# A transformer kernel on one core: the order of work in its segment attention, with the inputs turned one subblock ahead

## The chip, the core and the metric

The kernel runs on one core of a Trainium2 chip. TensorE (PE) does matrix products and transposes, VectorE (DVE), ScalarE (ACT) and GpSimd (POOL) do the work on elements, and SyncE (SP) issues the transfers. Each engine works through its own queue in order and waits on semaphores for the others. The metric is the time of one execution on the device in microseconds, median of three runs.

## The reference

Two sandwiched layers, each an attention and a mixture of experts, on `x` of 2 x 2048 x 128 in float32, every sublayer as `x = x + layernorm(f(layernorm(x)))`. The change touches the first sublayer only, attention in segments of 64 tokens, 16 heads of 64, with 16 persistent keys and values for each head. Shortened:

```python
xn = rmsnorm(x, norm_w)                       # x is layernorm of the input
q, k, v = split(xn @ w_qkv)                   # 16 heads of 64
q, k = rope(q), rope(k)
q_s, k_s, v_s = segments of 64 tokens
k_s = concat(pm_k, k_s); v_s = concat(pm_v, v_s)      # 80 keys
scores = einsum('bhid,bhjd->bhij', q_s, k_s) * 64 ** -0.5, masked causally
attn = softmax(scores)
out = einsum('bhij,bhjd->bhid', attn, v_s) @ w_out + b_out
x = x + layernorm(out)
```

## The kernel before

`local_attention` works through the 4096 tokens in 16 subblocks of 256 tokens (`NSUB`), each two query tiles of 128 tokens, tile 0 and tile 1 (`s` in the code). For a subblock it

- normalises the two tiles of inputs on DVE (`norm`, L336), turns them on PE into PSUM (`turn`, L544), and splits the result into a high part on ACT (`high`, L482) and a low part on DVE (`low`, L341), the buffers `xth` and `xtl`;
- makes four value products of 512 columns (`values_of`, L64 to L66), which ACT copies out of the bank (`values`, L504);
- makes eight projections, q and k of two head pairs at a time (`project`, L64 to L66). DVE multiplies each by cosine and sine (`rope`, L351), SP swaps odd and even rows by a transfer (L325), and POOL adds the two (`add`, L439 for q, L441 for k). A buffer ring of three ties rope `G` to addition `G-3`;
- makes scores for each tile in two halves of eight heads, called quads 0 and 1 (`scores`, L580 and L587). DVE takes their maxima (`maxes`, L358), ACT the exponentials, eight instructions for a quad (`exps`, L488), DVE the sum and its reciprocal (`softmax_back`, L365, L367). The division is shared: DVE does the upper 64 partitions (L371), POOL the lower 64 and the persistent keys (`normalise`, L448, L451), into `pb` and `ppm`;
- does, for each tile, seven *fills* of a PSUM bank (`fill`): transposes of the probabilities (kind `pt`, L605, L607) and products with the values (kind `ot`, L613), in the order pt0, pt1, ot0, pt2, pt3, ot1, pt4, numbered 0 to 6. ACT evacuates each (`evacuate`, L498). An eighth item is the output product (`out_project`, L624, L627). DVE reads it (`out_read`, L378 to L385), POOL takes the power (`power`, L457) and DVE finishes the layer norm and adds it to `X` (`finish`, L390, L394).

The work is a software pipeline written out by hand. In a step, every engine goes through one list in which three subblocks take part: `b` (live: values, projections, first scores), `a` (old, one behind: second scores, softmax, fills of tile 0) and `z` (older, two behind: fills of tile 1). `nxt` is the subblock after `b`, whose inputs are normalised and turned at the end of the step. The 16 fills and output products of a step and the turn share a ring of two banks (`fbank`). `place` and `place_x` number them in PE's order, 17 for a step, and `bank_released` makes each item wait until the item two places before it has been read. So the order on PE, the numbers and the waits hang together.

PE's list in a full step of the kernel before is: fill(z,1) 0; values 0, 1; fill 1; values 2, 3; projection 0; fills 2, 3; projection 1; fill 4; projection 2; fills 5, 6; projection 3; output product (z,1); scores (a,1,0); projection 4; scores (a,1,1); projection 5; fill(a,0) 0; projection 6; fill 1; projection 7; fills 2, 3, 4; scores (b,0,0); fills 5, 6; output product (a,0); turn of `nxt`; scores (b,0,1).

Of the kernel before, what the change touches and what calls it, by code (L numbers as in the profile page):

```python
# [5 lines left out]
F32 = mybir.dt.float32  # L6
# [7 lines left out]
P = 128  # L14
# [78 lines left out]
def local_attention(nc, dr, X, g):  # L93

    m = Mem(nc, "a_")
    with m:
# [125 lines left out]
                    last.then_inc(pm_mm, 1)  # L222

        xn = m.sb("xn", [P, ST, D])
        xth = m.sb("xth", [P, SUB], F32R)
        xtl = m.sb("xtl", [P, SUB], F32R)
        tr = m.sb("tr", [P, TRS, 2, 2, SUB])
        swp = m.sb("swp", [P, SWAPS, 2, SUB])
        qt = m.sb("qt", [P, 2, PAIRS, SUB])
# [45 lines left out]
        def par(n):  # L275
            return n % 2
# [6 lines left out]

        def place(n, s, i):

            return (n + 2) * ITEMS + i if s == 1 else (n + 1) * ITEMS + FILLS + 1 + i

        def place_x(n):
            return n * ITEMS - 1

        def turned_bank(n):
            return fbank[:, place_x(n) % 2, 0:SUB]
# [4 lines left out]
        def bank_released(eng, at):  # L297

            t, k = (at - 2) // ITEMS, (at - 2) % ITEMS
            if k == ITEMS - 1:  # L300
                if 0 <= t + 1 < NSUB:
                    eng.wait_ge(xtl_ready, t + 2)
                return
            n, s, i = (t - 2, 1, k) if k <= FILLS else (t - 1, 0, k - FILLS - 1)
            if 0 <= n < NSUB:
                if i == FILLS:
                    eng.wait_ge(y_read, n * ST + s + 1)
                else:
                    eng.wait_ge(fill_copied, (n * ST + s) * FILLS + i + 1)
# [6 lines left out]
        with nc.Block() as block:  # L316
# [13 lines left out]
            def _(dve):  # L330
# [7 lines left out]

                def low(b):
                    dve.wait_ge(xth_ready, b + 1)  # L340
                    nc.vector.tensor_tensor(xtl[:, :], turned_bank(b), xth[:, :].bitcast(F32),  # L341
                                            ALU.subtract).then_inc(xtl_ready, 1)

                def rope(b, *gs):
# [49 lines left out]
                    nc.vector.tensor_tensor(xs, xs, y[:, s, :], ALU.add).then_inc(y_fin, 1)  # L394

                norm(0)
                for b, a, z, nxt in steps:
                    live, old, older = b is not None, a is not None, z is not None
                    if live:
                        low(b)  # L400
                    if old:
                        maxes(a, 0, 0)
                        maxes(a, 0, 1)
                    if live:
                        rope(b, 0, 1)
                    if old:
                        softmax_back(a, 0)
                    if live:
                        rope(b, 2, 3)
                    if older:  # L410
                        finish(z, 0)
                        out_read(z, 1)
                    if old:
                        maxes(a, 1, 0)
                    if live:
                        rope(b, 4)
                    if old:
                        maxes(a, 1, 1)
                    if live:
                        rope(b, 5, 6, 7)  # L420
                    if nxt is not None:
                        norm(nxt)
                    if older:
                        finish(z, 1)
                    if old:
                        softmax_back(a, 1)
                        out_read(a, 0)

            @block.gpsimd
            def _(pool):  # L430
                def add(b, *gs):
                    for i in gs:
                        G = b * NG + i
                        kind, c = GROUPS[i]
                        pool.wait_ge(rope_mul, 2 * G + 2)
                        pool.wait_ge(swapped[G % SWAPS], 32 * (G // SWAPS + 1))
                        t0, t1 = tr[:, G % TRS, 0, :, :], swp[:, G % SWAPS, :, :]
                        if kind == "q":
                            nc.gpsimd.tensor_tensor(qt[:, par(b), 2 * c:2 * c + 2, :], t0, t1, ALU.add).then_inc(rope_add, 1)  # L439
                        else:  # L440
                            nc.gpsimd.tensor_tensor(kt[:, par(b), 2 * c:2 * c + 2, :, PM:KEYS0],  # L441
                                                    t0.rearrange("p c (a b) -> p c a b", b=SEG),
                                                    t1.rearrange("p c (a b) -> p c a b", b=SEG),
                                                    ALU.add).then_inc(rope_add, 1)

                def normalise(a, s):
                    pool.wait_ge(rden_done, a * ST + s + 1)
                    nc.gpsimd.tensor_tensor(pb[0:64, s, :, 0:SEG], e[0:64, s, :, PM:KEYS0],  # L448
                                            rden[0:64, s, :, None].to_broadcast([64, H0, SEG]),
                                            ALU.mult).then_inc(p_norm, 1)  # L450
                    nc.gpsimd.tensor_tensor(ppm[:, s, :].rearrange("p (h k) -> p h k", k=PM), e[:, s, :, 0:PM],  # L451
                                            rden[:, s, :, None].to_broadcast([P, H0, PM]),
                                            ALU.mult).then_inc(p_norm, 1)

                def power(a, s):
                    pool.wait_ge(y_chain, (a * ST + s + 1) * 3)
                    nc.gpsimd.tensor_tensor(yr[:, s:s + 1], yve[:, s:s + 1], eps[:, 0:1], ALU.pow).then_inc(y_pow, 1)  # L457

                nc.gpsimd.memset(pb[:, :, :, :], 0.0).then_inc(zeroed, 1)
                pool.wait_ge(zeroed, 1)  # L460
                for b, a, z, nxt in steps:
                    live, old, older = b is not None, a is not None, z is not None
                    if older:
                        power(z, 0)
                    if live:
                        add(b, 0, 1)
                    if old:
                        normalise(a, 0)
                    if live:
                        add(b, 2, 3)  # L470
                    if older:
                        power(z, 1)
                    if live:
                        add(b, 4, 5, 6, 7)
                    if old:
                        normalise(a, 1)

            @block.scalar
            def _(act):
                def high(b):  # L480
                    act.wait_ge(xt_mm, b + 1)
                    nc.scalar.activation(xth[:, :], turned_bank(b), ACT.Copy).then_inc(xth_ready, 1)  # L482

                def exps(a, s, j):
                    act.wait_ge(s_max, (a * ST + s) * QUADS + j + 1)
# [21 lines left out]
                high(0)  # L507
                for b, a, z, nxt in steps:
                    live, old, older = b is not None, a is not None, z is not None
                    if older:  # L510
                        evacuate(z, 1, 0)
                    if live:
                        values(b, 0)
                        values(b, 1)
                    if older:
                        evacuate(z, 1, 1)
                    if live:
                        values(b, 2)
                        values(b, 3)
                    if old:  # L520
                        exps(a, 0, 0)
                    if older:
                        evacuate(z, 1, 2, 3)
                    if old:
                        exps(a, 0, 1)
                    if older:
                        evacuate(z, 1, 4, 5, 6)
                    if old:
                        exps(a, 1, 0)
                        evacuate(a, 0, 0)  # L530
                        exps(a, 1, 1)
                        evacuate(a, 0, 1, 2, 3, 4, 5, 6)
                    if nxt is not None:
                        high(nxt)

            @block.tensor
            def _(pe):
# [9 lines left out]
                def values_of(b, c):  # L547
# [6 lines left out]
                        pe.wait_ge(v_copied, b * 2 * ST + c - 1)  # L554
                    ts = slice((c // 2) * P, (c // 2 + 1) * P)
                    vc = slice(2048 + (c % 2) * 512, 2048 + (c % 2) * 512 + 512)
                    matmul_split(nc, pbank[:, c % 2, :], xth[:, ts], xtl[:, ts], wh[:, vc], wl[:, vc]).then_inc(v_mm, 1)

                def project(b, i):
                    if i >= 2:  # L560
# [4 lines left out]
                    for half in range(2):  # L565
                        w0 = (1024 if kind == "k" else 0) + (2 * c + half) * P
                        last = matmul_split(nc, pbank[:, i % 2, half * SUB:(half + 1) * SUB], wh[:, w0:w0 + P],
                                            wl[:, w0:w0 + P], xth[:, :], xtl[:, :])
                    last.then_inc(proj_mm, 1)

                def scores(b, s, j):
# [58 lines left out]
                turn(0)  # L630
                for b, a, z, nxt in steps:
                    live, old, older = b is not None, a is not None, z is not None
                    if older:
                        fill(z, 1, 0)
                    if live:
                        values_of(b, 0)
                        values_of(b, 1)
                    if older:
                        fill(z, 1, 1)
                    if live:  # L640
                        values_of(b, 2)
                        values_of(b, 3)
                        project(b, 0)
                    if older:
                        fill(z, 1, 2, 3)
# [9 lines left out]
                        project(b, 3)  # L655
                    if older:
                        out_project(z, 1)
                    if old:
                        scores(a, 1, 0)
                    if live:  # L660
# [17 lines left out]
                    if old:  # L678
                        fill(a, 0, 5, 6)
                        out_project(a, 0)  # L680
                    if nxt is not None:
                        turn(nxt)
                    if live:
                        scores(b, 0, 1)

# [2783 lines left out]
```

## Time and profile before

| | us |
|---|---|
| runs | 2165.57, 2171.54, 2171.64 (median 2171.54) |
| span of the profiled execution | 2116.7 |
| its own total time | not printed by the page |
| steps of the segment attention | 13 full ones between 88 and 506 |
| busy over the span | PE 1765.5 (83%), DVE 1492.7 (71%), ACT 974.9 (46%), POOL 923.7 (44%) |

The page names one execution. The times of the runs are larger than its span since they hold what lies around it. PE counts as busy while its pipelined products are in flight, so neighbouring rows overlap by about 0.1 us. In a timeline row the bracket tells how long the engine stood idle before it and what released it.

### The profile page before, as it was taken

How to read it: one execution, taken by the hardware profiler on the slowest of the kernel's cores; microseconds unless marked ns; L12 is line 12 of the kernel's file. 1: busy time of each engine (PE TensorE's matmuls, PEld its weight loads, DVE VectorE, ACT ScalarE, POOL GpSimd, SP SyncE). 2: the span in 40 equal slices, each digit the busy share in tenths (PEclk: the TensorE clock that was granted, in tenths of full speed). 3: DMA queues.
4: the chain of work that ended last, by engine and by line, in shares of the span. 5: the costliest groups of instructions: out<-in, count | busy, mean ns of one | idle time of the engine just before them, and what ended most of it. 6: DMA issues, size and time to landing. Idle time of an engine off the chain costs nothing. (4 is left out here: it accounts for less than half of the span.)

```text
span 2116.7 us, 37485 instructions
## 1 busy us (share of the span) xinstructions
PE 1765.5 (83%) x13932; PEld 1331.8 (63%) x13932; DVE 1492.7 (71%) x3418; ACT 974.9 (46%) x2147; POOL 923.7 (44%) x637
## 2 busy tenths in 40 slices
PE   3788888888769999889999779965899779978993
PEld 2677777777635666446665557644688558767883
DVE  5678777787477887387787478878787776864234
ACT  2455545545415565525556345432333244325664
POOL 3455555565314566514555336654000220165644
PEclk9999999999859999979999889988899889988997
DMA  5112112111010000000000023319600000016763
GB/s 172 66 63 81 51 71 76 56 71 66 16 42 1 2 1 1 1 1 1 1 2 1 1 71 101 95 60 229 149 1 1 0 1 1 8 38 194 213 219 118
DMA packets 78469, 124.11 MB, mean 59 GB/s; under 512 B 11824, under 2 KB 43440, under 8 KB 77776
## 3 DMA queue, kind: packets, MB, share of 16 engines
q1 hardware_dynamic: 73744, 112.31, 17.1%
q0 software_dynamic: 4544, 9.41, 1.3%
q8 instruction: 111, 1.82, 0.4%
q14 instruction: 70, 0.57, 0.1%
HBM read 59.19 MB, written 28.94 MB: 42 GB/s over the span
## 5 line engine op out<-in xcount | busy, mean ns | idle before, releaser
L1089 POOL TENSOR_TENSOR mb_psum<-mb_pt 128x1024 f32<-128x1024 f32 x112 | 267.0, 2387 | 291.4 <-ACT mb_pt L1049 290.5
L1049 ACT ACTIVATE mb_pt<-mb_stb 128x1024 f32<-128x1024 f32 x256 | 249.2, 1021 | 143.2 <-PE mb_stb L1170 142.7
L914 DVE TENSOR_REDUCE mb_mxp<-mb_p1b 128x1 f32<-128x512 f32 x352 | 231.2, 684 | 50.2 <-PE mb_p1b L1154 46.3
L351 DVE TENSOR_TENSOR ma_tr<-ma_pbank,ma_cs 128x512 f32<-128x512 f32 x256 | 161.7, 683 | 91.4 <-PE ma_pbank L66 81.6
L488 ACT ACTIVATE ma_e<-ma_sbank,ma_mx 128x80 f32<-128x80 f32 x512 | 120.3, 385 | 99.0 <-DVE ma_mx L358 99.0
L2466 PE MATMUL mc_pv<-mc_pt,mc_v 128*128 128x256 f32 x544 | 148.2, 398 | 17.3 <-DVE mc_pt L2269 17.3
L1154 PE MATMUL mb_p1b<-mb_ks,mb_qs 96*128 96x512 f32 x352 | 151.3, 473 | 7.0 <-DVE mb_qs L907 3.3
L439 POOL TENSOR_TENSOR ma_qt<-ma_tr,ma_swp 128x512 f32<-128x512 f32 x64 | 82.3, 1289 | 167.8 <-DMA ma_swp<-ma_tr 167.7
L1170 PE MATMUL mb_stb<-mb_qs,mb_ks 98*128 98x512 f32 x512 | 143.8, 402 | 0.8 <-ACT mb_pt L1049 0.8
L2269 DVE COPY mc_pt<-mc_tb 128x512 f32<-128x512 f32 (+1 forms) x144 | 94.0, 658 | 61.5 <-PE mc_tb L2451 61.1
L1181 PE MATMUL mb_pvb<-mb_pt,mb_v 128*32 128x256 f32 x2048 | 137.0, 385 | 0.0
L1593 POOL TENSOR_TENSOR mb_hh<-mb_hh,mb_gb 128x512 f32<-128x512 f32 x64 | 98.7, 1545 | 82.8 <-DVE mb_hh L1610 55.4
L1756 POOL TENSOR_TENSOR mc_frs<-mc_fve,mc_half 128x4 f32<-128x4 f32 x8 | 8.1, 1012 | 275.5 <-DVE mc_fve L1740 275.4
L914 DVE TENSOR_REDUCE mb_mxp<-mb_misc 128x1 f32<-128x512 f32 x160 | 109.2, 682 | 22.0 <-PE mb_misc L1154 22.0
L2466 PEld LDWEIGHTS mc_pv<-mc_pt,mc_v 128*128 128x128 f32 x544 | 96.8, 196 | 35.3 <-DVE mc_pt L2269 25.8
L1170 PEld LDWEIGHTS mb_stb<-mb_qs,mb_ks 98*128 98x128 f32 x512 | 94.2, 189 | 33.2 <-issue 12.3
L498 ACT ACTIVATE ma_pt<-ma_fbank 128x512 f32<-128x512 f32 (+1 forms) x160 | 94.2, 590 | 42.2 <-PE ma_fbank L605 41.8
L64 PE MATMUL ma_pbank<-ma_xth,ma_wh 128*128 128x256 f32 x256 | 85.6, 334 | 30.0 <-DVE ma_tr L351 30.0
L1154 PEld LDWEIGHTS mb_p1b<-mb_ks,mb_qs 96*128 96x128 f32 x352 | 67.4, 199 | 67.8 <-DVE mb_mxp L914 48.2
L448 POOL TENSOR_TENSOR ma_pb<-ma_e,ma_rden 64x1024 f32<-64x1024 f32 x32 | 90.1, 2817 | 31.6 <-DVE ma_rden L367 31.6
L613 PE MATMUL ma_fbank<-ma_pt,ma_v 128*64 128x128 f32 x1024 | 73.6, 287 | 35.3 <-ACT ma_pt L498 35.2
L441 POOL TENSOR_TENSOR ma_kt<-ma_tr,ma_swp 128x512 f32<-128x512 f32 x64 | 83.6, 1316 | 39.0 <-DMA ma_swp<-ma_tr 34.6
(404 smaller groups left out, 4767.2 us busy)
## 6 DMA issues: line engine op xcount, KB each, us to landing
ma_swp<-ma_tr SPq DMA_DIRECT2D x256, 128.0 KB, 2.0
md_wslot<-d_weights SPq DMA_DIRECT2D x39, 516.0 KB
d_xs<-mw_blank SPq DMA_DIRECT2D x1, 16899.0 KB, 72.3
mb_gb<-b_gates SPq DMA_DIRECT2D x64, 256.0 KB, 3.2
md_xs<-d_xs SPq DMA_DIRECT2D x39, 131.0 KB, 3.3
md_work<-d_ret SPq DMA_DIRECT2D x8, 512.0 KB, 5.4
mg_X<-x SPq DMA_DIRECT2D x4, 512.0 KB, 9.8
ma_cs<-cs SPq DMA_DIRECT2D x1, 2048.0 KB, 9.9
```

The source lines that it names most:

```text
L351: nc.vector.tensor_tensor(tr[:, G % TRS, part, :, :], pbank[:, i % 2, :].rearrange("p (c t) -> p c t", c=2), cs[:, b // 2, part, None, :]. ...
L488: nc.scalar.activation(e[:, s, slot, :], sbank[:, 2 * j + k // 4, k % 4 * KEYS0:(k % 4 + 1) * KEYS0], ACT.Exp, bias=mx[:, s, slot:slot + 1 ...
L498: nc.scalar.activation(to[:, 4 * q:4 * q + nh, :], filled_bank(a, s, i)[:, 0:nh * P].rearrange("p (a b) -> p a b", b=P), ACT.Copy).then_in ...
L914: nc.vector.tensor_reduce(mxp[:, r // NCH, r % NCH:r % NCH + 1], pass_bank(r), AXX, ALU.max).then_inc(p1_max, 1)
L1049: nc.scalar.activation(pt[:, T % RING, :, :].rearrange("p (b h) q -> p b (h q)", b=2), stb[:, 2 * (i % 2):2 * (i % 2) + 2, :], ACT.Exp, sc ...
L1089: nc.gpsimd.tensor_tensor(psum[:, n % SUMS, :, :], pt[:, T % RING, :, :], pt[:, (T + 1) % RING, :, :], ALU.add).then_inc(summed, 1)
L1154: nc.tensor.matmul(pass_bank(r), qs[V % 3][0:QROWS, h, t * P:(t + 1) * P], ks[0:QROWS, c * BLK:(c + 1) * BLK], start=True, stop=True).then ...
L1170: last = nc.tensor.matmul(stb[:, 2 * (i % 2) + hp, :], ks[:, i * P:(i + 1) * P], qs[U % 3][:, 2 * hp:2 * hp + 2, :].rearrange("p h q -> p ...
L1181: last = nc.tensor.matmul(pvb[h * DK:(h + 1) * DK, 0:UQ], v1[:, i, :], pt[:, T % RING, h, :], start=(i == 0), stop=(i == KT - 1), skip_gro ...
L1593: nc.gpsimd.tensor_tensor(hh[:, t % HR, :], hh[:, t % HR, :], gb[:, q % GBR, :], ALU.mult).then_inc(gated, 1)
L2269: nc.vector.tensor_copy(pt[:, K % 2, 0:wd], tb[:, K % 2, 0:wd]).then_inc(pt_copied, 1)
L2466: last = nc.tensor.matmul(pv[:, 0:HC * P], v[:, t, :], pt[:, K % 2, a * HC * P:(a + 1) * HC * P], start=(t == 0), stop=(t == r))
```

## The change

The buffers `xth` and `xtl` are doubled, and the parity of the subblock chooses the half. The turn of the next subblock goes from the end of the step to the place behind the output product of tile 1, and its number in the ring with it. The order on each engine changes:

- PE: fill(z,1) 0 stands behind values 0 and 1, and fill 1 behind values 2 and 3; the turn behind the output product (z,1). The rest stays.
- ACT: evacuations 0 and 1 of (z,1) behind the copies of values 1 and 3; evacuation 4 ahead of the exponentials (a,0,1); the high part ahead of the exponentials (a,1,0).
- DVE: the norm of `nxt` and the finish of (z,0) behind the first maxima; rope 2 ahead of the softmax part of (a,0); the low part behind the read of (z,1).
- POOL: addition 2 ahead of normalising (a,0).

```diff
-        xth = m.sb("xth", [P, SUB], F32R)
-        xtl = m.sb("xtl", [P, SUB], F32R)
+        xth = m.sb("xth", [P, 2, SUB], F32R)
+        xtl = m.sb("xtl", [P, 2, SUB], F32R)
...
-            return (n + 2) * ITEMS + i if s == 1 else (n + 1) * ITEMS + FILLS + 1 + i
+            return (n + 2) * ITEMS + i if s == 1 else (n + 1) * ITEMS + FILLS + 2 + i
 
         def place_x(n):
-            return n * ITEMS - 1
+            return (n - 1) * ITEMS + FILLS + 1
...
             t, k = (at - 2) // ITEMS, (at - 2) % ITEMS
-            if k == ITEMS - 1:
+            if k == FILLS + 1:
                 if 0 <= t + 1 < NSUB:
                     eng.wait_ge(xtl_ready, t + 2)
                 return
-            n, s, i = (t - 2, 1, k) if k <= FILLS else (t - 1, 0, k - FILLS - 1)
+            n, s, i = (t - 2, 1, k) if k <= FILLS else (t - 1, 0, k - FILLS - 2)
... (DVE)
                 norm(0)
+                low(0)
                 for b, a, z, nxt in steps:
-                    if live:
-                        low(b)
                     if old:
                         maxes(a, 0, 0)
                         maxes(a, 0, 1)
+                    if nxt is not None:
+                        norm(nxt)
+                    if older:
+                        finish(z, 0)
                     if live:
-                        rope(b, 0, 1)
+                        rope(b, 0, 1, 2)
                     if old:
                         softmax_back(a, 0)
                     if live:
-                        rope(b, 2, 3)
+                        rope(b, 3)
                     if older:
-                        finish(z, 0)
                         out_read(z, 1)
+                    if nxt is not None:
+                        low(nxt)
                     if old:
                         maxes(a, 1, 0)
...
                         rope(b, 5, 6, 7)
-                    if nxt is not None:
-                        norm(nxt)
                     if older:
                         finish(z, 1)
... (POOL)
-                        add(b, 0, 1)
+                        add(b, 0, 1, 2)
                     if old:
                         normalise(a, 0)
                     if live:
-                        add(b, 2, 3)
+                        add(b, 3)
... (ACT)
-                    if older:
-                        evacuate(z, 1, 0)
                     if live:
                         values(b, 0)
                         values(b, 1)
                     if older:
-                        evacuate(z, 1, 1)
+                        evacuate(z, 1, 0)
                     if live:
                         values(b, 2)
                         values(b, 3)
+                    if older:
+                        evacuate(z, 1, 1)
                     if old:
                         exps(a, 0, 0)
                     if older:
-                        evacuate(z, 1, 2, 3)
+                        evacuate(z, 1, 2, 3, 4)
                     if old:
                         exps(a, 0, 1)
                     if older:
-                        evacuate(z, 1, 4, 5, 6)
+                        evacuate(z, 1, 5, 6)
+                    if nxt is not None:
+                        high(nxt)
                     if old:
                         exps(a, 1, 0)
                         evacuate(a, 0, 0)
                         exps(a, 1, 1)
                         evacuate(a, 0, 1, 2, 3, 4, 5, 6)
-                    if nxt is not None:
-                        high(nxt)
... (PE)
-                    if older:
-                        fill(z, 1, 0)
                     if live:
                         values_of(b, 0)
                         values_of(b, 1)
                     if older:
-                        fill(z, 1, 1)
+                        fill(z, 1, 0)
                     if live:
                         values_of(b, 2)
                         values_of(b, 3)
+                    if older:
+                        fill(z, 1, 1)
+                    if live:
                         project(b, 0)
...
                         out_project(z, 1)
+                    if nxt is not None:
+                        turn(nxt)
...
                         out_project(a, 0)
-                    if nxt is not None:
-                        turn(nxt)
```

## Rows read from the trace of the kernel before

**Rows 1.** Windows between input copies: bounds, length, busy PE, PEld, DVE, ACT, POOL, clock, DMA

```profile
88.00:120.00 32.00, 28.62 (x358) 24.32 (x354) 24.43 (x42) 16.95 (x52) 17.54 (x14) 0.95 0.18 68
...
376.70:409.30 32.60, 27.00 (x350) 22.98 (x350) 25.75 (x41) 16.86 (x51) 18.10 (x15) 1.00 0.18 66
...
474.50:506.10 31.60, 27.08 (x350) 23.07 (x350) 25.54 (x42) 16.92 (x52) 17.19 (x15) 1.00 0.18 68
```

**Rows 2.** Waits from 88 to 506 us: total, times, longest

```profile
PE ma_fbank L613 <- ACT ma_pt L498: 23.4, 25, 1.3
...
PE ma_fbank L605 <- POOL ma_ppm L451: 14.2, 11, 1.6
```

**Rows 3.** Timeline of PE, one step: start, busy, what, idle before and its releaser

```profile
376.25 0.38 PE L544 MATMUL ma_fbank<-mg_ident,ma_xn 128*128 128x128 f32 x2
...
379.05 0.66 PE L605 MATMUL ma_fbank<-mg_ident,ma_pb 128*128 128x128 f32 x4 [1.61 <-POOL ma_ppm L451]
379.46 0.48 PE L64 MATMUL ma_pbank<-ma_wh,ma_xth 128*128 128x512 f32 x1
...
380.94 0.60 PE L605 MATMUL ma_fbank<-mg_ident,ma_pb 128*128 128x128 f32 x4
...
382.92 0.39 PE L64 MATMUL ma_pbank<-ma_xth,ma_wh 128*128 128x256 f32 x1
...
388.65 1.09 PE L613 MATMUL ma_fbank<-ma_pt,ma_v 128*64 128x128 f32 x16 [1.30 <-ACT ma_pt L498]
...
390.67 1.95 PE L624 MATMUL ma_fbank<-ma_wout,ma_ot 128*128 128x128 f32 x16
...
393.00 0.33 PE L580 MATMUL ma_sbank<-ma_mask,mg_identb 64*64 64x320 bf16 x4
```

**Rows 4.** Timeline of DVE, the same step

```profile
377.64 0.42 DVE L341 TENSOR_TENSOR ma_xtl<-ma_fbank,ma_xth 128x256 fp32r<-128x256 f32 x1
...
383.93 1.29 DVE L351 TENSOR_TENSOR ma_tr<-ma_pbank,ma_cs 128x512 f32<-128x512 f32 x2 [4.42 <-PE ma_pbank L66]
...
388.05 1.49 DVE L365 TENSOR_REDUCE ma_den<-ma_e 128x16 f32<-128x1280 f32 x1 [0.51 <-ACT ma_e L488]
...
389.86 2.17 DVE L371 TENSOR_TENSOR ma_pb<-ma_e,ma_rden 64x1024 f32<-64x1024 f32 x1
...
395.04 0.28 DVE L378 TENSOR_TENSOR ma_y<-ma_fbank,ma_bout 128x128 f32<-128x128 f32 x1
...
395.98 0.82 DVE L358 TENSOR_REDUCE ma_mx<-ma_sbank 128x8 f32<-128x640 f32 x1
...
402.74 1.97 DVE L336 TENSOR_SCALAR ma_xn<-mg_X,ma_mean,ma_xsc 128x128 f32<-128x128 f32 x2
```

**Rows 5.** Timeline of ACT, the same step

```profile
380.44 1.30 ACT L504 ACTIVATE ma_v<-ma_pbank 128x512 f32<-128x512 f32 x2
...
383.46 1.84 ACT L488 ACTIVATE ma_e<-ma_sbank,ma_mx 128x80 f32<-128x80 f32 x8
...
386.09 1.93 ACT L488 ACTIVATE ma_e<-ma_sbank,ma_mx 128x80 f32<-128x80 f32 x8
387.77 0.74 ACT L498 ACTIVATE ma_pt<-ma_fbank 128x512 f32<-128x512 f32 x1
```

**Rows 6.** Timeline of POOL, the same step

```profile
387.40 1.27 POOL L439 TENSOR_TENSOR ma_qt<-ma_tr,ma_swp 128x512 f32<-128x512 f32 x1 [7.90 <-DMA ma_swp<-ma_tr]
389.67 1.27 POOL L439 TENSOR_TENSOR ma_qt<-ma_tr,ma_swp 128x512 f32<-128x512 f32 x1 [1.00 <-DMA ma_swp<-ma_tr]
...
393.76 0.61 POOL L451 TENSOR_TENSOR ma_ppm<-ma_e,ma_rden 128x256 f32<-128x256 f32 x1
```

**Rows 7.** All instructions of L336, of L371 and of L448: duration ns min/median/max

```profile
L336 DVE TENSOR_SCALAR ma_xn<-mg_X,ma_mean,ma_xsc x32: 334/700/3545, 29.8 to 500.0; 128x128 f32<-128x128 f32 x32
...
L371 DVE TENSOR_TENSOR ma_pb<-ma_e,ma_rden x32: 1221/1418/2179, 69.2 to 561.8; 64x1024 f32<-64x1024 f32 x32
...
L448 POOL TENSOR_TENSOR ma_pb<-ma_e,ma_rden x32: 1892/2896/2942, 70.1 to 561.9; 64x1024 f32<-64x1024 f32 x32
```

## The prediction before the run

> **What bounds the kernel now.** I read four views, in this order. First the windows, cut at the ScalarE copies of the turned input, one per step. Between 88.0 and 506.1 us there are 13 full steps, 418.1 us together, 32.16 on average; most take 32.6, the others 31 to 32 [rows 1]. In none is an engine full: in the step from 376.7, PE works 27.0 us of 32.6 and DVE 25.8. A pipeline like that is bound by a loop of waits. PEclk is 1.00 there, so the clock doesn't explain it.
>
> Then the waits [rows 2]. PE waits for POOL's normalised probabilities, 14.2 us in 11 waits, and for ScalarE's copies of transposed probabilities, 23.4 in 25. The timeline places them. I count from A, the start of the turn at 376.25 us, which follows the output product. The next A is 32.6 later.
>
> - Turn and last scores end at 377.44 (A+1.19); then PE idles 1.61 until the first fill of tile 1 at A+2.80. Value products, a fill between them, and projection 0, which starts at A+6.67, follow [rows 3].
> - DVE, idle 4.42 meanwhile, starts rope 0 at A+7.68 [rows 4].
> - ScalarE ends the exponentials of tile 0, quad 1, at 388.02 (A+11.77) [rows 5]. That frees DVE's softmax back part at A+11.80; its multiply into `pb` takes 2.17 because POOL is adding at that moment [rows 4, 6]. Rope 2 and 3, finish and read follow, and the maxima of tile 1, quad 0, start at A+19.73.
> - From there DVE, ScalarE and PE hand over with small gaps to the next A, 408.85-395.98 = 12.87 later.
>
> DVE also works 1.97 on the next inputs' norm at 402.74, before the softmax part whose result the first fill awaits [rows 4].
>
> The 31.6 steps are those in which that first fill comes about 1 us sooner. So in a long step the loop runs: A, first fill, values, projection 0, rope 0, softmax back, maxima (1,0), exponentials, fills of tile 0, output product, A.
>
> **The change, part by part.** Durations and pitches (start to start) are those of the rows; the clock starts at A again. Nothing is added: the buffers double, the instructions are the same.
>
> *Opening of PE.* The turn goes from here (0.38 busy) to behind the output product of tile 1, and the first fill goes behind two value products. Scores run 0 to 0.81, values 0 and 1 to 2.29 (379.46 to 380.94 is 1.48 for two), fill 0 to 2.70, values 2 and 3 to 4.18, fill 1 to 4.59. Projection 0 is ready 1.01 after its start (382.92 to 383.93): A+5.60, against A+7.68. Copies don't hold it up: the first two end 2.28 after the first value product starts (A+3.09), the next two at A+4.98, and each product awaits a copy that ended before.
>
> Does the first fill still wait? Its data are ready at A+2.80 less hand-over today. With the norm (1.97) gone from in front of that softmax part they come near A+0.9; they are wanted at A+2.29. Margin 1.4.
>
> *ScalarE.* After the copies: evacuation 1 to 5.57, eight exponentials to 7.25 (the next starts 1.68 after them, 386.09 to 387.77), evacuations 2 and 3 to 8.2 (0.95 for two today, 383.46 + 1.68 = 385.14 to 386.09). Evacuation 4 now stands before the second eight. PE: fill 2 starts when evacuation 1 ends, 5.65 to 6.68, fill 3 to 7.09, projection 1 ready at 8.10, fill 4 behind it at 8.65. So evacuation 4 runs 8.69 to 9.29, the exponentials 9.15 to 11.05. They end 0.7 sooner than now, not 2.08: that is the price of evacuation 4 in front. From A+1.79 to A+11.05 ScalarE would work 2.4 + 3.0 + 3.6 = 9.0 of 9.26 us, nearly full. In exchange fill 5 no longer waits 1.30 for evacuation 4 behind the exponentials [rows 3, 5]: the output product of tile 1 can start at 11.6 instead of A+14.42.
>
> *DVE.* Rope 0 at 5.63, rope 1 at 8.12, rope 2, now before the softmax part, 9.42 to 10.7. It fits in the wait for the exponentials, so it costs nothing; without that cover, 1.24. Softmax back from 11.08, its multiply at 12.89. POOL adds rope 0 from 9.1 (lag 3.47, 383.93 to 387.40), rope 1 from 11.5, rope 2 from 12.85. The multiply again meets an addition: 2.17, so 15.1; the ends are 1.22 and about 2.5 (1.22 behind a whole addition of 1.27) [rows 6, 7]. I take 2.17, the row with the same collision. Rope 3 to 16.3. Finish, 0.58 until the read, has gone; reading the output product takes 0.94 (395.04 to 395.98), the low part of the turned inputs 0.42. Maxima (1,0) start at A+17.65, 2.1 sooner.
>
> *What was moved to the opening*, norm and finish of tile 0, follows the first maxima, A+2.6 to A+3.9; rope 0 wants DVE at 5.63. Cover 1.7 us. POOL is idle then, so the norms should take 0.33 rather than up to 1.4 each [rows 7]; even two at 1.4 fit, nearly.
>
> *The moved turn.* Output product 11.6 to 13.93 (390.67 to 393.00 is 2.33), turn to 14.3, ScalarE's high part to 14.7. Waiting instructions: the high part, with exponentials (1,0) queued behind it, wanted at 18.5; the low part on DVE, with the maxima (1,0) behind it, reached at 17.2. Margin 2.5. Fill 1 (A+4.2) now waits for DVE's read of the last output product, done near A+0.4: no cost.
>
> *POOL and SP.* POOL normalises tile 0 behind the third addition: 14.1 to 17.6 (2.90 and 0.61). PE asks at 17.7 and would next wait for rope 4 anyway until 19.6: cover 2.0. SP's swaps keep their order and lag; an addition of rope G-3 frees each slot in time, as before.
>
> *Sum.* The stretch from the maxima on keeps its 12.87: the new step is 17.65 + 12.87 = 30.5, for all steps alike, since the late first fill of the 32.6 us steps no longer decides. Per step 32.16 - 30.5 = 1.65; 13 steps 21.4. The step after 506.1, and the one behind it in which evacuation 4 frees the last output product sooner, I count as one gain each (estimate): 3.3. The head, two steps without a full pipeline, 0. Sum 24.7. The profiled span goes from 2116.7 to about 2092. The page prints only the span; the runs lie 48.9 to 54.9 above it, their median 54.8. I subtract from the median: 2171.5 - 24.7 = 2147.
>
> **A rule weighed.** The multiply takes 1.22 to 2.18 and its POOL partner 1.89 or 2.9, so one stands while the other works [rows 6, 7]. The Trainium skill, "SBUF — State Buffer", section "Who interferes with whom", says that a VectorE instruction with two SBUF inputs contends with a GpSimd instruction that reads SBUF, and that whichever starts first holds the shared ports for its whole length. By that rule this change is delicate: if the third addition starts first, the multiply takes up to 2.49, and the sum is 14 x 0.32 = 4.5 us worse, 2151; if the multiply starts first it runs free, which is the first rival below, 2134. The trace agrees with it in both lengths.
>
> **Rivals.**
> 1. *The multiply gets ahead of the third addition.* My sum has them 0.04 us apart (12.89 and 12.85), far below its accuracy. The multiply then takes 1.22, 0.95 less, and POOL's wait is covered. 14 steps: 13 more, 2134. Against: all POOL additions slide with the same ropes, and in 12 of the 13 steps today's multiply of tile 0 takes over 2.1 (one such row stands). Chance 0.13.
> 2. *Only the late first fill goes.* Every step becomes what the short ones are, 31.6, and no more, because exponentials (0,1) or the evacuations bind at the old distance. 0.56 in each of 15 steps: 8.4, so 2163. For: that is a time the trace shows. Against: the turn and fill 0 leave PE's opening as well. Chance 0.15.
> 3. *ScalarE's queue binds, and the kernel is slower.* One place: evacuation 4 in front of exponentials (0,1). It waits for fill 4, which stands on PE behind projection 1 and fill 2, which wait for evacuations 1 and 2 of the same queue. Any lateness goes round this ring and straight into the softmax part. A slip of the exponentials' start from 9.15 by 1.65 takes the whole gain; from there on it is a loss, and at 2.3 it is 15 x 0.65 = 10 us: 2181. For: the queue is 97% full by my sum. Against: its copies take 0.60 in every row and depend on nothing that got later; they would need a third more. Slower 0.08; a slip of 1.2 to 2.1, no measurable change, 0.09.
> 4. *The change doesn't do what it says*, since the turn arrives late and DVE stands at the low part: from an output product at 14.1 on, 1 us for each. It starts at A+14.42 today, so even with evacuation 4 of no use it would cost only 0.3 a step. It is inside my range.
>
> **How the numbers follow.** The forecast has 0.55, with its own range 2138 to 2158 (0.6 to 2.2 us a step). Rival 1 gives 2134, rival 2 2163 to 2166. The range is 2133 to 2166. A difference of 0.3%, 6.5 us, is about what a measurement of this kernel can tell from none: faster means under 2165. Faster: 0.55 + 0.13 + two thirds of 0.15 = 0.78; same: the rest of rival 2 and 0.09 = 0.14; slower 0.08.
>
> **What would show it.** The 13 steps all near 30.5 us, without the 31.6/32.6 mix. PE's wait for POOL's `ppm` before the fills gone. The norms at 0.33, right behind the first maxima. DVE's softmax multiply at 2.17 (1.22 is rival 1). PE's 1.30 wait for evacuation 4 gone, output product of tile 1 near A+11.6. Wrong would be: ScalarE idle before evacuation 4 by over 1 us, DVE's wait before the sum of exponentials over 1 us (rival 3), DVE waiting at the low part (rival 4), or a PEclk under 0.97 in these steps.

## The result, and the profile after

| | before | changed |
|---|---|---|
| runs | 2170.86 us (2165.57 to 2171.64) | 2132.09 us (2124.59 to 2136.96) |
| ratio | | 0.9822, 95% interval 0.9804 to 0.9841 |
| first attention ends, in the trace | 581.7 | 541.9 |
| mean of the 12 steps between rope 0 of subblocks 3 and 15 | 32.31 | 29.47 |

The change is worth 39 us, and the trace has all of it, 39.8 us, in the part that was changed. Forecast were 2147 and a range from 2133: right in sign, too small, and 0.9 us outside the range. The number that came is that of the first rival, 2134.

One warning on the spans: the changed kernel's profiled span is 2135.2 us, longer than the 2116.7 of before. The profiled run took 2136.96, so only 1.8 us lie around a span. The profile of before was of an execution some 50 us quicker than the timed ones. Its last two parts, which the change doesn't touch, have the lengths that the quicker chips show (last section). Within the first attention the two traces compare. So the reason given ahead of the prediction, that the runs are longer than the span by what lies around it, was wrong.

Windows of the changed kernel, cut at the input copies as in [rows 1], with the same columns:

```profile
101.80:131.10 29.30, 27.20 (x348) 23.22 (x346) 24.31 (x41) 16.79 (x51) 18.09 (x15) 1.00 0.20 74
307.70:337.40 29.70, 27.61 (x352) 23.58 (x350) 24.11 (x42) 16.78 (x51) 18.57 (x15) 1.00 0.19 72
425.90:455.30 29.40, 27.33 (x348) 23.29 (x347) 23.81 (x42) 16.79 (x51) 18.26 (x15) 1.00 0.20 74
```

Steps are nearly all alike, 29.4, and PE works as long as before in each, 27.2 to 27.6 us, now 93% of it. DVE needs 23.8 to 24.3 in these three windows, against 25.8 in the one from 376.7 before, for the same instructions: less of its time is spent waiting on POOL inside an instruction. Of the waits of [rows 2] PE's for `ppm` fell from 14.2 to 2.5 us, the one for the copies from 23.4 to 7.5 (here from 102 to 455 us, 12 steps against 13):

```profile
PE ma_fbank L615 <- ACT ma_pt L500: 7.5, 12, 1.0
...
PE ma_fbank L607 <- POOL ma_ppm L453: 2.5, 3, 1.2
```

Now one step in time. The line numbers of ACT, POOL and PE are 2 higher than before. A, where the last scores start on PE, is 323.54 (352.90, the next one, less 29.36). DVE first; its rows answer to [rows 4]:

```profile
326.06 0.59 DVE L336 TENSOR_SCALAR ma_xn<-mg_X,ma_mean,ma_xsc 128x128 f32<-128x128 f32 x2
...
329.05 1.29 DVE L351 TENSOR_TENSOR ma_tr<-ma_pbank,ma_cs 128x512 f32<-128x512 f32 x2 [1.81 <-PE ma_pbank L66]
331.56 2.48 DVE L351 TENSOR_TENSOR ma_tr<-ma_pbank,ma_cs 128x512 f32<-128x512 f32 x4 [1.22 <-PE ma_pbank L66]
334.37 1.49 DVE L365 TENSOR_REDUCE ma_den<-ma_e 128x16 f32<-128x1280 f32 x1 [0.32 <-ACT ma_e L490]
...
336.18 1.22 DVE L371 TENSOR_TENSOR ma_pb<-ma_e,ma_rden 64x1024 f32<-64x1024 f32 x1
...
339.90 0.82 DVE L358 TENSOR_REDUCE ma_mx<-ma_sbank 128x8 f32<-128x640 f32 x1
```

PE, ACT and POOL in the same step, the answers to [rows 3], [rows 5] and [rows 6]:

```profile
332.74 1.09 PE L615 MATMUL ma_fbank<-ma_pt,ma_v 128*64 128x128 f32 x16
...
334.97 2.02 PE L626 MATMUL ma_fbank<-ma_wout,ma_ot 128*128 128x128 f32 x16
...
352.90 0.33 PE L582 MATMUL ma_sbank<-ma_mask,mg_identb 64*64 64x320 bf16 x4
...
355.21 0.60 PE L607 MATMUL ma_fbank<-mg_ident,ma_pb 128*128 128x128 f32 x4
```

```profile
332.00 0.60 ACT L500 ACTIVATE ma_pt<-ma_fbank 128x512 f32<-128x512 f32 x1 [0.30 <-PE ma_fbank L607]
332.49 1.85 ACT L490 ACTIVATE ma_e<-ma_sbank,ma_mx 128x80 f32<-128x80 f32 x8
```

```profile
336.27 2.26 POOL L443 TENSOR_TENSOR ma_kt<-ma_tr,ma_swp 128x512 f32<-128x512 f32 x1
...
353.25 0.61 POOL L453 TENSOR_TENSOR ma_ppm<-ma_e,ma_rden 128x256 f32<-128x256 f32 x1
```

The point to see is the pair 336.18 and 336.27. DVE's multiply starts 0.09 us before POOL's addition 2. It runs free, 1.22 us, and it is the addition that takes 2.26 instead of 1.27. In [rows 4, 6] it was the other way round.

### The profile page after: what moved, and what is told of

Its sections match the earlier page's. It is cut to its first block and busy times, and to the rows that moved or that the text cites. A ratio compares the mean times of both kernels' runs of the same rounds, so it can differ in the third digit from the quotient of the medians.

```text
span 2135.2 us, 37484 instructions
## 1 busy us (share of the span) xinstructions
PE 1782.7 (83%) x13932; PEld 1340.9 (63%) x13932; DVE 1469.6 (69%) x3418; ACT 973.7 (46%) x2147; POOL 920.9 (43%) x637
## 5 line engine op out<-in xcount | busy, mean ns | idle before, releaser
L3326 PE MATMUL md_bk<-md_xT,md_wslot 128*128 128x256 f32 x312 | 99.5, 404 | 13.7 <-issue 10.9
L3112 POOL DMA_INDIRECT d_ret<-md_ys,md_home x78 | 76.8, 985 | 78.4 <-DVE md_ys L3245 65.0
L443 POOL TENSOR_TENSOR ma_kt<-ma_tr,ma_swp 128x512 f32<-128x512 f32 x64 | 96.8, 1516 | 23.6 <-DMA ma_swp<-ma_tr 18.6
L3056 ACT ACTIVATE md_a<-md_bk,md_wslot 128x256 f32<-128x256 f32 x156 | 70.6, 477 | 73.8 <-PE md_bk L3326 26.3
```

The source lines that it names most:

```text
L3326: nc.tensor.matmul(ub[:, c, :], wslot[:, j % WRING, c * P:(c + 1) * P], xT[:, j % 2, :], start=True, stop=True).then_inc(up_mm, 1)
```

## The experiments

The experiments ran on four chips, each beside the kernel before; ratios compare, microseconds across the two kinds of chip (last section) don't. "Step" is the mean of the same 12 steps as above, in one trace; in brackets the commonest single step, or the range of most.

| kernel | step | ratio (interval) |
|---|---|---|
| before | 32.31 (32.6) | 1 |
| changed; again in E12 | 29.47; 29.43 (29.36) | 0.9822; 0.9819 (0.9789 to 0.9849) |
| E1 multiply waits for addition 2 | 33.30 (32.5 to 33.6) | 1.0101 (1.0074 to 1.0128) |
| E9 multiply 0.4 us later | 30.62 (30.6) | 0.9884 (0.9856 to 0.9913) |
| E2 norm back | 29.71 (29.8) | 0.9853 (0.9832 to 0.9873) |
| E3 rope 2 back | 30.67 (30.55) | 0.9914 (0.9894 to 0.9935) |
| E4 evacuation 4 back | 29.52 (29.5) | 0.9830 (0.9810 to 0.9851) |
| E7 turn back | 29.82 (29.8) | 0.9834 (0.9785 to 0.9882) |
| E13 fills back | 29.93 (29.7) | 0.9864 (0.9826 to 0.9902) |
| E6 before, addition 1 held | 33.73 (32.6 to 34.6) | 1.0100 (1.0048 to 1.0152) |
| E10 before, finish ahead | 31.33 (30.9 to 32.0) | 0.9950 (0.9920 to 0.9979) |
| E11 before, both | 30.52 (30.0 to 31.1) | 0.9892 (0.9864 to 0.9920) |
| E8, E14 fill 1 ahead | 28.84; 28.88 (28.75) | 0.9754; 0.9779 |
| E15 and low part behind | 28.86 (28.75) | 0.9784 (0.9739 to 0.9829) |

The intervals of E2, E4, E7 and E13 overlap with that of the changed kernel. What is said of them rests on the steps, which the two traces of the changed kernel repeat to 0.04 us.

**E1.** One wait in front of the multiply of tile 0.

```diff
+                    if s == 0 and a + 1 < NSUB:
+                        dve.wait_ge(rope_add, (a + 1) * NG + 3)
```

> The changed kernel, with one wait more: DVE's multiply of tile 0 into pb waits until POOL has ended addition 2 (rope 2). So the collision that I had forecast is brought back as a full wait. Theory (this multiply stands on the loop that sets the step; it ran free at 1.22 us, and that is the 1 us a step that my sum lacked): the multiply starts near A+14.1 instead of A+12.63, the step goes from 29.4 to 30.8 us, the kernel from 2132 to about 2152. Rival (this place has slack and the gain came from elsewhere): step 29.4, time 2132.

The time was 2188 us, a loss of 56 and not 20. DVE and then POOL:

```profile
373.45 2.84 DVE L373 TENSOR_TENSOR ma_pb<-ma_e,ma_rden 64x1024 f32<-64x1024 f32 x1 [1.50 <-POOL ma_kt L445]
```

```profile
372.08 1.27 POOL L445 TENSOR_TENSOR ma_kt<-ma_tr,ma_swp 128x512 f32<-128x512 f32 x1
373.31 1.90 POOL L452 TENSOR_TENSOR ma_pb<-ma_e,ma_rden 64x1024 f32<-64x1024 f32 x1
```

When the wait lets DVE go, POOL has begun to normalise 0.14 us before, and the multiply stands behind that as well. Counted from rope 0 (364.85), it ends at 11.44; in the changed kernel (329.05) at 8.35. That is 3.09 later, and the step without another collision went from 29.36 to 32.5, by 3.1. So the direction of the theory holds, one for one; its size missed since I had not looked at what POOL does next.

**E5 and E9.** The multiply is delayed by small instructions that read the sums and write a spare tile: one in E5, three in E9.

```diff
+                    if s == 0:
+                        for k in range(3):
+                            nc.vector.reciprocal(rdx[:, k, :], den[:, s, :])
```

> The changed kernel, with one small DVE instruction more (the reciprocal of tile 0's sums once again into a spare tile, 0.29 us with its gap) right in front of the multiply of tile 0. In the changed kernel the multiply starts at A+12.63 and POOL's addition 2 at A+12.73. Theory (who starts first decides, and my forecast had the wrong one first by 0.1 us): the multiply now asks after addition 2 has begun and takes 2.2 to 2.3 us, 1.22 before; the step goes from 29.4 by 0.29 + 1.0 to 30.7, near the 30.5 of my forecast, and the kernel by 14 x 1.3 = 18 us to 2150. Rival (the overlap is not decided so sharply, DVE has precedence): multiply 1.22, step 29.65, +4 us.

E5 didn't bring the collision about: ratio 0.9835 (0.9785 to 0.9886), step 29.51. The extra instruction overlaps the one before and delayed the multiply by 0.1 us, not 0.29. DVE stayed first, by 0.02 us. DVE, then POOL:

```profile
367.57 1.22 DVE L374 TENSOR_TENSOR ma_pb<-ma_e,ma_rden 64x1024 f32<-64x1024 f32 x1
```

```profile
367.59 2.35 POOL L446 TENSOR_TENSOR ma_kt<-ma_tr,ma_swp 128x512 f32<-128x512 f32 x1
```

> The changed kernel, with three small DVE instructions in front of the multiply of tile 0 (the reciprocal of the sums three times into a spare tile). One such instruction delayed the multiply by 0.1 us only, and it was still first, by 0.02 us. Three should delay it by 0.5, behind the start of POOL's addition 2. Theory (who starts first decides): the multiply takes about 2.0 us, ends 1.1 to 1.3 later than in the changed kernel, step 30.6, the kernel +16 us. Rival (DVE has precedence, or the overlap is graded): multiply 1.22, step 29.36 + 0.5 = 29.9, +7 us.

In E9 the multiply starts 0.21 us behind the addition. DVE, then POOL:

```profile
347.42 2.14 DVE L375 TENSOR_TENSOR ma_pb<-ma_e,ma_rden 64x1024 f32<-64x1024 f32 x1
```

```profile
347.21 1.26 POOL L447 TENSOR_TENSOR ma_kt<-ma_tr,ma_swp 128x512 f32<-128x512 f32 x1
```

Step 30.6, as the theory had it; the rival's 29.9 is out. Counted from rope 0, the multiply starts 0.33 us later than in the changed kernel and ends 1.25 later, and the step is 1.25 longer: 0.33 is the delay, 0.92 the collision. In time, on one chip, E9 took 2146.1 us and the changed kernel (E12) 2130.4, where the theory had 16 us. The run holds a control of its own: where two multiplies happened to get through in 1.22 us the step took 29.7 and 30.2, though a step of 31.5 followed the second. This kernel, the changed one with the collision of my forecast and the multiply at about the start that I had given it, has the step of my forecast (30.5).

**E2, E3, E4, E7, E13** undo one part each.

E2 (DVE) and E3 (DVE, and the same on POOL):

```diff
+                norm(1)
...
-                    if nxt is not None:
-                        norm(nxt)
...
                         rope(b, 5, 6, 7)
+                    if b is not None and b + 2 < NSUB:
+                        norm(b + 2)
```

```diff
-                        rope(b, 0, 1, 2)
+                        rope(b, 0, 1)
...
-                        rope(b, 3)
+                        rope(b, 2, 3)
```

> The changed kernel, with DVE's norm of the inputs back behind rope 7, ahead of finish and softmax part of tile 1 (for the subblock after next, so the early turn stays). Theory (the move of the norm freed the first fill): POOL's results for the first fill come near A+2.9 instead of A+0.96, PE wants them at A+2.3: a wait of 0.6 us comes back, step 30.0, kernel +9 us. Rival (the norm's place is covered on both sides, the gain is all of the rope 2 and softmax part): step 29.4, no change.

> The changed kernel, with rope 2 on DVE and addition 2 on POOL back behind the softmax part of tile 0. Theory (rope 2 fills the wait for the exponentials, so its place is worth its whole length): DVE idles about 1.5 us before the sum of exponentials and does rope 2 on the loop, step 29.4 + 1.2 = 30.6, kernel +17 us; the multiply stays near 1.22 to 1.3, since addition 1 ends about when it starts. Rival (only the multiply's luck matters): the multiply free as well, step 29.4. A third reading, that addition 1 now collides with the multiply: multiply about 2.2, step 31.5.

The norm's place is worth 0.25 (mean) to 0.45 us (commonest step), under the 0.6 expected, though more than the rival's nothing. Rope 2's place is worth its length: 1.19 in the commonest step. DVE idles 19.7 us in 13 waits before the sum of exponentials, 1.5 each, where it idled 0.32.

E4 (ACT) and E7 (turn, high and low part, ring numbers as before; the turn stands here for all three):

```diff
-                        evacuate(z, 1, 2, 3, 4)
+                        evacuate(z, 1, 2, 3)
...
-                        evacuate(z, 1, 5, 6)
+                        evacuate(z, 1, 4, 5, 6)
```

```diff
                         out_project(a, 0)
+                    if nxt is not None:
+                        turn(nxt)
```

> The changed kernel, with evacuation 4 of tile 1 back behind the exponentials of tile 0, quad 1. Theory: two ends meet here. Exponentials end 0.6 us sooner, but DVE then starts only 0.3 sooner, behind rope 2; the output product of tile 1 starts at A+12.65 instead of A+11.4 and its result is read by DVE at A+15.1, when DVE comes anyway. Step 29.4 within 0.2, kernel the same. Rival (the early evacuation is what brought the gain): step over 30, kernel +8 us or more. Other rival (it costs, as my working had it, 0.6 us of exponentials): step 29.1 or less, -4 us.

> The changed kernel, with the turn, its high part on ScalarE and low part on DVE back where they stood before, at the end of the step (ring numbers too), the norm and all other orders as changed. Theory: the turn (0.31) stands on PE's opening again and the value products wait for the low part, which DVE has ready near A+1.9 rather than for nothing from A+0.85: projection 0 comes 1.0 to 1.1 us later, step 30.5, kernel +14 us. Rival (the turn early is worth only its own 0.31, since the first fill fills the gap): step 29.7, +4 us.

E4: no change in time, 0.15 in the step, as the theory forecast, but not for its reason. DVE, then POOL:

```profile
337.39 1.59 DVE L371 TENSOR_TENSOR ma_pb<-ma_e,ma_rden 64x1024 f32<-64x1024 f32 x1
```

```profile
336.61 1.29 POOL L441 TENSOR_TENSOR ma_qt<-ma_tr,ma_swp 128x512 f32<-128x512 f32 x1 [0.56 <-DMA ma_swp<-ma_tr]
337.92 2.21 POOL L443 TENSOR_TENSOR ma_kt<-ma_tr,ma_swp 128x512 f32<-128x512 f32 x1
```

The multiply starts 0.42 us sooner after rope 0 than in the changed kernel, 6.71 instead of 7.13. There it meets the last 0.5 us of addition 1, takes 1.59, and ends at 8.30 instead of 8.35. So a collision eats what the later evacuation gives the exponentials, and E4 doesn't say what evacuation 4 in front costs by itself.

E7 lost 0.44, nearer to the rival's answer: rope 0 comes 0.7 us later after the output product, but without the low part the stretch between the multiply and the maxima is 0.3 shorter. I had added up only one side in this expectation.

E13 puts fill(z,1) 0 ahead of the value products and fill 1 between them, with their evacuations:

> The changed kernel with the first two fills of tile 1 (and their evacuations) back where they stood: fill 0 ahead of the value products, fill 1 between them. The early turn and all else stay. Theory (with the norm out of the way POOL's results come 1.4 us before PE wants them, so the spreading only permutes items of equal length): step 29.4 within 0.2, no change. Rival (the spreading brought part of the gain, since evacuation 0 now stands ahead of the value copies and the third value product waits): step 29.8 or more, +5 us.

0.33 us in the commonest step, 0.5 on the mean, and PE's waits for `ppm` are back in some: 7.9 us in 15 waits (2.5 in 3). The theory's "no change" is out. The mean step, 29.93, is the rival's, the commonest, 29.7, just under it: the spreading by itself is worth a little.

**E6, E10, E11** do parts in the kernel before. E6 on POOL, E10 on DVE, E11 both:

```diff
-                        add(b, 0, 1)
+                        add(b, 0)
+                    if old:
+                        pool.wait_ge(p_norm_high, a * ST + 1)
+                    if live:
+                        add(b, 1)
```

```diff
                         maxes(a, 0, 1)
+                    if older:
+                        finish(z, 0)
...
-                        finish(z, 0)
                         out_read(z, 1)
```

> The kernel before, with POOL's addition 1 held until DVE's multiply of tile 0 has ended (a wait on its semaphore; order otherwise the same). Theory (in the kernel before this multiply stood on the loop as well, and its collision cost 0.95 us in nearly every step): multiply 1.22 instead of 2.17, the step 32.28 to 31.3, the kernel -12 to -13 us, about 2156. Rival (before, the loop ran through other places, the collision was covered): step 32.3, no change, or slower because addition 1 comes 1.4 us later.

E6 was slower, 1.0100, against the theory. The rival had allowed for it, by the later addition; the rows show more than that. DVE, then POOL:

```profile
401.30 1.22 DVE L371 TENSOR_TENSOR ma_pb<-ma_e,ma_rden 64x1024 f32<-64x1024 f32 x1
402.55 2.48 DVE L351 TENSOR_TENSOR ma_tr<-ma_pbank,ma_cs 128x512 f32<-128x512 f32 x4
404.95 0.86 DVE L390 TENSOR_SCALAR ma_y<-ma_y,ma_ymv,ma_yr 128x128 f32<-128x128 f32 x1
405.84 3.08 DVE L394 TENSOR_TENSOR mg_X<-mg_X,ma_y 128x128 f32<-128x128 f32 x1
```

```profile
402.60 1.27 POOL L439 TENSOR_TENSOR ma_qt<-ma_tr,ma_swp 128x512 f32<-128x512 f32 x1 [2.54 <-DVE ma_pb L371]
403.83 1.90 POOL L448 TENSOR_TENSOR ma_pb<-ma_e,ma_rden 64x1024 f32<-64x1024 f32 x1
405.69 0.62 POOL L451 TENSOR_TENSOR ma_ppm<-ma_e,ma_rden 128x256 f32<-128x256 f32 x1
406.27 2.50 POOL L441 TENSOR_TENSOR ma_kt<-ma_tr,ma_swp 128x512 f32<-128x512 f32 x2
```

The multiply is free, but POOL's work is now one row without a pause, 402.60 to 408.77, and the finish, 0.6 us alone, sits in it for 3.9 us. That gives a new theory for each of two runs:

> The kernel before with one part of the change: DVE's finish of tile 0 (two instructions, 0.6 us) behind the first maxima instead of between rope 3 and the read of the output product. Theory (the stretch from the multiply to the maxima of tile 1 is on the loop, 1 for 1): step 32.28 to 31.65, the kernel -8 us. Rival (in the kernel before, other waits cover it): no change.

> The kernel before with POOL's addition 1 held until the multiply of tile 0 has ended, and DVE's finish of tile 0 behind the first maxima. Held alone, the addition made the multiply free but the finish met POOL's unbroken row of normalise and additions and took 3.9 us instead of 0.6. Theory (the two collisions are the whole reason): with the finish out of the way the step is 32.28 - 0.95 - 0.6 = 30.7, the kernel about -20 us. Rival (holding the addition costs of itself, by later additions): step over 32.

E11 bears the theory out: 30.52 against 30.7, and 22 us less, while the edits alone gave +25 and -9. With the finish out of POOL's row, the held addition is good for 0.8 us a step (31.33 to 30.52). E10 gained 0.98, more than the finish's 0.6. The traces show where the rest lies: the maxima (1,0) follow rope 0 by 11.45 us instead of 12.03 (medians of 12 steps), and in the opening too POOL's `ppm` is ready 0.6 sooner behind the output product, 2.41 instead of 3.01, and rope 0 with it.

**E12** is the changed kernel once more.

> The changed kernel again, so that it stands beside the others on one chip. Every theory: ratio to the kernel before 0.982 within 0.003, step 29.4 to 29.5.

**E8, E14, E15**, further than the change. E8 and E14 are one kernel; PE, then ACT:

```diff
-                        fill(a, 0, 0)
+                        fill(a, 0, 0, 1)
```

```diff
-                        evacuate(a, 0, 0)
+                        evacuate(a, 0, 0, 1)
                         exps(a, 1, 1)
-                        evacuate(a, 0, 1, 2, 3, 4, 5, 6)
+                        evacuate(a, 0, 2, 3, 4, 5, 6)
```

> A trial to go further: the changed kernel, with fill 1 of tile 0 ahead of projection 6 on PE and its evacuation ahead of the exponentials of tile 1, quad 1, on ScalarE. Theory (the tail of the loop runs exponentials (1,1), evacuation 1, fill 2, ..., output product): fill 2 no longer waits for evacuation 1 behind the exponentials, starts 0.5 us sooner, behind projection 7; step 28.9, kernel -7 us, 2125. Rival (the exponentials, 0.5 later, or projection 7 bind instead): step 29.4, no change.

> The trial with fill 1 of tile 0 and its evacuation ahead once more, to stand on one chip with the others: step 28.7 to 28.9, ratio 0.976 to the kernel before.

E15 moves DVE's `low(nxt)` behind `maxes(a, 1, 0)` on top of it.

> The same with DVE's low part of the turned inputs behind the maxima of tile 1, quad 0, instead of ahead of them. Theory (the stretch from the multiply to these maxima is on the loop 1 for 1): 0.33 us less, step 28.4, the kernel -4 to -5 us against the trial before. Rival (exponentials (1,0), or rope 4 behind the low part, bind at the old time): step 28.75.

Fill 1 ahead takes 0.6 us off the step on two chips. The ratios 0.9754 and 0.9779 lie below the changed kernel's 0.9822 and 0.9819, which ran on other chips, but their intervals overlap or nearly touch; the step is the sharper sign. With E15, which equals it, it is the fastest version here. E15 gave nothing: with fill 2 no longer behind the exponentials, PE waits 0.95 us for rope 5 ahead of projection 7, and rope 5 comes at the same time wherever the low part stands before it. In the changed kernel the stretch to the maxima counted one for one when it grew (E1, E3, E9) and when it shrank (the 0.3 us of E7); in E8's kernel shrinking it no longer helps.

## Why the prediction was wrong

The loop was the right one, and its steps can be set against the trace (A = 323.54):

| | forecast | trace |
|---|---|---|
| rope 0 | A+5.63 | A+5.51 |
| evacuation 4, exponentials (0,1) | 8.69, 9.15 | 8.46, 8.95 |
| output product, tile 1 | 11.6 | 11.43 |
| `ppm` of tile 1 ready, fill 0 wants it | 0.9, 2.29 | 0.96, 2.31 |
| multiply starts; addition 2 starts | 12.89; 12.85 | 12.64; 12.73 |
| multiply takes | 2.17 | 1.22 |
| maxima (1,0) | 17.65 | 16.36 |
| step | 30.5 | 29.36 |

**The step that failed** is "The multiply again meets an addition: 2.17, so 15.1". The mechanism was named, and rival 1 gave its price and the time that was measured. What was wrong is the choice between two starts that my own sum had 0.04 us apart. It came out 0.09 the other way, E5 left DVE first by 0.02 with no loss, and in E9, with DVE 0.21 behind, the step was 30.6. That shows both that the order of the starts decides and that this one length is the shortfall: 0.95 of the 1.2 us a step. The other 0.25 is the multiply's earlier start, from exponentials that began 0.2 sooner than in my sum. (The maxima came 1.29 sooner than forecast in all, and the stretch behind them took 13.00 instead of 12.87.) The 12.85 was itself loosely worked: with my lag of 3.47 behind rope 2 at 9.42, addition 2 starts at 12.89, exactly with the multiply. My argument against rival 1, that today's multiply collides in 12 of 13 steps, carried nothing: then it met addition 1, now addition 2, with another lag. It deserved near one half, and the range a lower end.

**Right**, by its own step: the first fill's wait went, its margin is 1.35 us (forecast 1.4), and E2 shows it coming back in part. Rope 2 is hidden (E3: 1.19, forecast 1.24). What evacuation 4 in front costs is not shown: a collision covers it in E4. Norm and finish in the opening ran at 0.3 us each, with 1.8 us of DVE idle left (forecast 1.7). The turn arrived in time. PEclk stayed at 1.00.

**Rivals 2 to 4.** Rival 2's 31.6 did not come. Rival 3: ScalarE is as full as said, but idles only 0.30 ahead of evacuation 4. Rival 4: the high part is ready 1.5 us before DVE's low part.

**The arithmetic.** 2.83 us a step over 13 steps (32.29 to 29.46, rope 0 of subblock 2 to that of 15) is 36.8 us; the tail gave 2.8 more, the head 0.2. I had taken 32.16 for today's step. For the tail I had two gains of 1.65, 3.3; it gave one gain of the real size, so that the two figures are near each other is luck. The sentence that the runs lie 48.9 to 54.9 above the span because of what surrounds it was wrong: that is 1.8 us. It did no harm, since the sum was a difference.

The port rule cited ahead of the run, from the Trainium skill, "SBUF — State Buffer", section "Who interferes with whom", says that the instruction which starts first keeps the shared ports for its whole length. E5 and E9, 0.02 and 0.21 us either side, agree with it, and so do all other multiplies traced here (last section).

## What to carry to other kernels

If your sum puts two instructions of DVE and POOL that take both operands from SBUF within a few tenths of a microsecond, you don't know which one pays: give both outcomes equal weight, and set the range by them. Then look at what stands behind: who was first decides whether the engine on the loop or the one with slack stretches. And don't cure one collision by holding an engine back before you have followed its whole row; E1 and E6 each removed an overlap and met a longer one.

## What the runs showed of the hardware

- The order of the starts decides sharply, and the wait can be reckoned. The 17 traces hold 544 of DVE's multiplies into `pb`. Where DVE started first, even by 0.004 us (E5), it took 1.22. Where a POOL instruction was running already, it took that instruction's remaining time plus 1.08, and never less than 1.22: 2.31 when DVE was 0.04 behind the start of a 1.27 us addition (once in the changed kernel), 2.14 at 0.21 behind (E9), 1.56 at 0.80 behind (E4). Being late by nearly the whole addition costs nothing, being late by a hair costs most.
- A DVE instruction of 0.3 us can be held much longer than one POOL instruction. In E6 the 128x128 addition took 3.08 us beside three POOL instructions in a row, although in the kernel before and in E9 the multiply got in behind a single one while POOL had more work waiting. Why it gets in at one place and not at the other is open.
- The chips differ. The kernel before took 2169 us on two of them and 2117 to 2119 on two others. The third and fourth part take 465 to 471 and 211 to 214 us in the traces of the quicker kind, 496 to 500 and 232 to 235 in those of the slower, where the mean granted clock of these parts is also lower (0.89 to 0.90 and 0.83 to 0.84, against 0.91 to 0.93 and 0.87). Which of the two brings the other, or whether a third thing does, is not shown. The second part takes 843 to 850 us on both. The first part can't be compared across the kinds, since no kernel was traced on both. Two traces of the changed kernel on slower chips agree in it to 0.1 us, E8's and E14's on quicker ones differ by 5.3. A span is to be compared with runs of its own chip alone.
